# Order of instructions at three stage fronts of a one-core decoder kernel: gates of the last network moved up, attention's turned rows copied ahead of the next rows, query stack cleared behind the constants

## What is computed

```python
x = x + attn(layernorm(x))            # L0, L1: causal, 16 heads of 8, rotary; L2: channel attention; L3: state space
x = x + xattn(layernorm(x), ctx)      # L0 (gated), L1, L3: 16 heads over the context; L2: decay mixing
x = x + ffn(layernorm(x))             # L0, L1, L2: one of 8 experts per token
                                      # L3: shared network plus 2 of 8 small experts, by sigmoid scores
```

## Time and profile before

| what | value |
|---|---|
| median of 3 runs | 1519.24 us (1514.60 to 1520.48) |
| profiled execution, its own time | 1520.62 us |
| its span in the trace | 1518.8 us, 30086 instructions |
| PE, DVE, ACT, POOL busy | 78%, 64%, 42%, 39% of the span |
| granted clock of PE, mean | 0.871 |

### The profile page before, as it was taken

One profiled execution on the slowest core, in us unless ns is written; L12 is line 12 of the kernel. 1 busy time (PEld: TensorE's weight loads), 2 busy tenths in 40 slices (PEclk: granted clock), 3 DMA queues, 4 the chain that ended last, 5 costly groups with the idle time before them and its releaser, 6 DMA issues. The chain is left out here.

```text
span 1518.8 us, 30086 instructions
## 1 busy us (share of the span) xinstructions
PE 1187.3 (78%) x9187; PEld 788.5 (52%) x9187; DVE 977.1 (64%) x4100; ACT 640.3 (42%) x1541; POOL 597.9 (39%) x1132
## 2 busy tenths in 40 slices
PE   3789999998465478999997495874758865999778
PEld 2456555554365245565553394663655642454455
DVE  6677777774666567787772674456665755775445
ACT  2256555444222135566654043331335431666422
POOL 3554478987243344355520443322430122321120
PEclk8699999999578579999999597876887886999889
DMA  6344765530022344455420125001220014331000
GB/s 187 111 131 126 218 198 166 182 116 12 32 60 62 98 125 127 134 172 166 148 93 12 41 57 177 0 15 38 62 74 1 0 39 146 99 121 39 2 0 28
DMA packets 140015, 137.35 MB, mean 90 GB/s; under 512 B 12289, under 2 KB 109185, under 8 KB 139729
## 3 DMA queue, kind: packets, MB, share of 16 engines
q1 hardware_dynamic: 131248, 110.88, 24.0%
q0 software_dynamic: 8608, 24.55, 5.0%
HBM read 83.58 MB, written 49.18 MB: 87 GB/s over the span
## 5 line engine op out<-in xcount | busy, mean ns | idle before, releaser
L763 ACT ACTIVATE L0a_Pr<-PS 128x512 f32<-128x512 f32 (+1 forms) x256 | 137.0, 547 | 140.5 <-PE PS L665 86.4
L763 ACT ACTIVATE L1a_Pr<-PS 128x512 f32<-128x512 f32 (+1 forms) x256 | 136.2, 548 | 104.1 <-PE PS L662 51.6
L480 POOL TENSOR_TENSOR L0a_PG<-L0a_Pr,L0a_G 128x512 f32<-128x512 f32 x80 | 105.8, 1326 | 23.6 <-issue 10.4
L886 DVE CUSTOM_DVE_ANT_0 L1a_junk<-PS,L1a_neg 128x256 bf16<-128x256 f32 x256 | 94.8, 420 | 29.4 <-PE PS L638 29.1
L638 PE MATMUL PS<-L1a_Kst,Qm 128*128 128x256 bf16 (+1 forms) x512 | 94.6, 272 | 16.4 <-DVE L1a_mx L886 8.6
L638 PE MATMUL PS<-L0a_Kst,Qm 128*128 128x256 bf16 (+1 forms) x512 | 94.7, 272 | 16.1 <-DVE L0a_mx L886 9.2
L886 DVE CUSTOM_DVE_ANT_0 L1a_junk<-PS,causal_q 128x128 bf16<-128x128 f32 (+1 forms) x256 | 78.4, 353 | 38.4 <-PE PS L638 37.6
L886 DVE CUSTOM_DVE_ANT_0 L0a_junk<-PS,causal_q 128x128 bf16<-128x128 f32 (+1 forms) x256 | 78.4, 353 | 38.1 <-PE PS L638 37.5
L660 PE MATMUL PS<-Qm,L0a_Kst 128*128 128x512 bf16 (+1 forms) x256 | 91.2, 356 | 12.2 <-DMA Qm<-L0a_mT 9.5
L660 PE MATMUL PS<-Qm,L1a_Kst 128*128 128x512 bf16 (+1 forms) x256 | 91.2, 356 | 10.5 <-DMA Qm<-L1a_mT 7.3
L889 DVE TENSOR_REDUCE L3x_mx<-PS 128x2 f32<-128x512 f32 x128 | 83.6, 687 | 24.2 <-PE PS L638 23.7
(11 more groups left out here) (739 smaller groups left out, 3189.8 us busy)
## 6 DMA issues: line engine op xcount, KB each, us to landing
Qm<-q_image SPq DMA_DIRECT2D x160, 128.0 KB
sorted_in<-zeros POOLq DMA_DIRECT2D x16, 516.0 KB, 4.3
L0a_Kst<-k_image SPq DMA_DIRECT2D x64, 128.0 KB
ffn_w_<-L_ffn POOLq DMA_DIRECT2D x32, 256.0 KB, 3.5
L1a_Kst<-k_image SPq DMA_DIRECT2D x64, 128.0 KB
ffn_w_<-L_ffn SPq DMA_DIRECT2D x16, 256.0 KB, 6.5
L3x_Kst<-k_image SPq DMA_DIRECT2D x32, 128.0 KB
k_image<-L0a_kpart SPq DMA_DIRECT2D x16, 192.0 KB, 2.5
```

The source lines that it names most:

```text
L480: g.tensor_tensor(PG[:, V_ % GATED_RING, :].rearrange("p (h q) -> p h q", h=2), Pr[:, V_ % RING, :].rearrange("p (h q) -> p h q", h=2), G[ ...
L763: a(Pr[:, V_ % RING, 0:2 * nq], PS[:, T_BANK + v % 2, 0:2 * nq], ACT.Exp, scale=SCALE)\
L886: ins = v.tensor_tensor_reduce(junk[:, tt, par, 0:nk], scored[:, par], off, 1.0, LOWEST, ALU.add, ALU.max, mx[:, i % 2, tt, par, hp:hp + 1])
```

## The change

Three edits of order; no instruction is added or removed. In attention, ACT's copy of the turned rows (XT+1) stands ahead of the writing of normalised rows (NORM+1) within a slot. In the first pass, DVE's second clear of Qm moves from its first instructions to behind the constants. In the last network the fourth turn moves from unit 5 to unit 4, the gate products from units 2, 4, 6, 7 to 2, 3, 4, 5, and the exponential from before unit 9 to before unit 7.

```diff
--- before.py
+++ after.py
@@ -785,6 +785,12 @@
                         if i >= RUNS:
                             act.wait_ge(s["xn_ready"], i - RUNS + 1)
                         a(r0[:, i % RUNS], lnv[:, i % RUNS], ACT.Exp, scale=-0.5).then_inc(s["ln_r0"], 1)
+                    i = at(n, XT + 1)
+                    if i is not None:
+                        act.wait_ge(s["xT_psum"], i + 1)
+                        if i >= DEPTH:
+                            act.wait_ge(s["v_psum"], i - DEPTH + 1)
+                        a(xT[:, i % DEPTH], PS[:, f_bank(XT), 0:S], ACT.Copy).then_inc(s["xT_ready"], 1)
                     i = at(n, NORM + 1)
                     if i is not None:
                         act.wait_ge(s["ln_scale"], i + 1)
@@ -794,12 +800,6 @@
                             ins = a(xn[:, i % 2, t, :], tile(items[i][1], t), ACT.Identity, scale=rstd[:, i % RUNS, t:t + 1],
                                     bias=shift[:, i % RUNS, t:t + 1])
                         ins.then_inc(s["xn_ready"], 1)
-                    i = at(n, XT + 1)
-                    if i is not None:
-                        act.wait_ge(s["xT_psum"], i + 1)
-                        if i >= DEPTH:
-                            act.wait_ge(s["v_psum"], i - DEPTH + 1)
-                        a(xT[:, i % DEPTH], PS[:, f_bank(XT), 0:S], ACT.Copy).then_inc(s["xT_ready"], 1)
                     i = at(n, K + 1)
                     if i is not None and items[i][0] not in ROPE:
                         first_part(i, "k", f_bank(K))
@@ -904,7 +904,6 @@
 
                 if first:
                     v.memset(Qm[0:64, :, 1], 0.0).then_inc(s["setup"], 1)
-                    v.memset(Qm[64:P, :, 0], 0.0).then_inc(s["setup"], 1)
                 for n in SLOTS:
                     if first and n == CONSTS:
                         dve.wait_ge(s["w_in"], 16)
@@ -912,6 +911,7 @@
                             v.tensor_copy(to[:, :], w(name))
                         v.memset(core.causal_q[:, 0:P], 0.0)
                         v.tensor_copy(core.causal_q[:, P:S], w("neg_q")).then_inc(s["consts"], 1)
+                        v.memset(Qm[64:P, :, 0], 0.0).then_inc(s["setup"], 1)
                     i, u = unit(n, 0)
                     if i is not None:
                         if first and i == 0 and u == 0:
@@ -2313,9 +2313,9 @@
     N = len(units)
     count = lambda kind, n: sum(1 for u in units[:n] if u[0] == kind)
     nth = lambda kind, g, k: units.index((kind, g, k))
-    TURN_AT = {1: 1, 3: 2, 5: 3}
-    GATE_AT = {2: 0, 4: 1, 6: 2, 7: 3}
-    SIGMOID_AT = 9
+    TURN_AT = {1: 1, 3: 2, 4: 3}
+    GATE_AT = {2: 0, 3: 1, 4: 2, 5: 3}
+    SIGMOID_AT = 7
     MASK_AT = {nth(SHARED, 2, NE - 1): 0, nth(ROUTED, 0, 1): 1, nth(ROUTED, 1, 1): 2, nth(ROUTED, 2, 1): 3}
     spread = [("mask", g) if x == "mask" else ("pick", x) for n in range(N) for x, g in
               ([(n, None)] if units[n][0] == ROUTED else []) + ([("mask", MASK_AT[n])] if n in MASK_AT else [])]
```

## The result

The changed kernel took 1506.94 us (median of 5 runs, 1506.00 to 1511.05), the kernel before 1519.32 beside it (5 runs, 1514.60 to 1520.48): a ratio of 0.9929, 95% interval 0.9909 to 0.9950. Forecast were 1509.4 and 1503.5 to 1516.0, and "faster by over 0.5%" had the largest chance. A later comparison of 9 runs with 18 of the kernel before gave 0.9943 (0.9923 to 0.9963), a third 0.9939 (0.9922 to 0.9956).

What follows compares the result with a forecast made beforehand. Bound: a chain of barrier-separated stages, where one engine's order holds back a ready product at each front. Terms 4.66+2.05+1.46+1.70=9.87 off the profiled 1520.62 make 1510.8; from the median, 1509.4, range 1503.5 to 1516.0.

Steps and rivals of the forecast that it cites:

- First front, 4.66 forecast: First pass: item 0's copy of turned rows at 9.66 instead of 14.32, 4.66 earlier, by moved clear and copy order.
- the statistics can start at 4.75, the 0.70 of idle stays: First pass, DVE: first statistics start where the memset did, 2.65 earlier, with the idle before it kept.
- the forecast's second sentence: First pass: statistics could even start at 4.05, 3.35 earlier, but POOL, on its table until after 5.89, could hardly follow.
- The clear's new place, 0 forecast: First pass: memset behind the constants delays neither item 2's statistics nor POOL's normalising; price 0, bound a loss of 2.45.
- Second network, 2.05 forecast: Second network's attention front: copy of turned rows ahead of item 1's rows gives 2.05, bounds 1.9 to 2.1.
- L3x, 1.46 forecast: L3x front: key's first part (L753) 1.46 earlier, still behind item 1's rows and a logarithm of 0.21; bounds 1.2 and 2.07.
- Last network, 1.70 forecast: Last network: routing starts 3.0 earlier, 1.3 lost to POOL's multiplies, so 1.7 gained; bounds 0.9 and 3.0.
- The walk against POOL's cadence: Last network's routing: POOL's multiplies, every 1.75, hold L2514 by 0.8 and the second L2511 by 0.5, 1.3 lost.
- The turn's wait: Last network: fourth transpose, now behind unit 4, waits 0.5 for DVE's rows; bounds 0 and 1.2.
- I leave the half clock as it is.: Last network: PE still idles about 5.0, over the 4.3 after which the clock fell, so no gain was counted.
- The rivals: Clock stays up: 1506.6 (0.12); first front gives half: 1510.4 to 1511.9 (0.12); pass swallows front: 1517.5 (0.12); slower pass: 1527 (0.06).
- the slower rival: First pass stays at half clock, keyed products 0.63 instead of 0.36; at 41 us delay 7.7 slower, 1527; chance 0.06.

## Why the prediction was right, and where its steps were off

- **First front, 4.66 forecast.** The first key product came 4.75 earlier and the image writes 4.76; the pass's fifteenth item of sixteen ended 4.57 earlier (376.28 to 371.71). The step "the statistics can start at 4.75, the 0.70 of idle stays" was off: they started at 3.98, because that idle belongs to the clear and moved with it. It hardly mattered, as the forecast's second sentence said: POOL was still on its table (6.14), so that the rows came 2.78 earlier, 0.13 beyond the 2.65. The wait ahead of the rows grew from 1.76 to 2.47.
- **The clear's new place, 0 forecast.** Right: item 2's statistics at 9.98 wait for x's load; L451 and L452 are at their 0.20 and 0.22 beside it.
- **The rest of L0a.** The pass ended 6.65 earlier in the profiled pair and 5.86 on the mean of the traces, not 4.66. The 2.1 that came on top in the pair arose between the fifteenth item's end and the sixteenth's, where the kernel before had dropped to half clock (0.74 over 376 to 388 us) and the changed one dropped only at 379.7, with its last item's products done. Over all twelve traces the fifteenth item ended 5.0 earlier, and from there to the sixteenth's end it took 8.0 or 9.6 to 10.1, in both kinds. The other 0.9 of the 5.86 is how often the long one came. No term of the sum had it.
- **Second network, 2.05 forecast.** 2.04 at the image write, 2.05 on the mean of traces.
- **L3x, 1.46 forecast.** L753 came 1.59 nearer: the logarithm that follows item 1's rows held it 0.09, not 0.21. On the mean of traces the stage gave 1.27; in the profiled one nothing, with 54.8 of half clock for 44.3.
- **Last network, 1.70 forecast.** L2401 came 1.81 nearer (38.78 after the stage's start, from 40.59). The walk against POOL's cadence was right in both places and sizes: 0.78 at L2514 and 0.52 at the second L2511, together 1.30. The turn's wait was 0.32 for 0.5, and the idle 5.00 as forecast.
- **"I leave the half clock as it is."** That step was off. The clock fell where it had (37.3 after the stage's start, 37.6 before) but rose after 6.8, not 10.2, and 5.4 after L2401 in place of 7.3. So one unit of the routed work ran at half, where in the kernel before a part of the next did too (its product began with 1.21 and ended with 0.63). It comes with edit 3: the half clock there lasted 10.2 in all four traces without edit 3, and 6.8 in all five that have it and nothing added there. It gave 0.86 more in the profiled pair (2.67 for the stage, 1.81 at L2401), and 0.5 more on the means (2.33 for the stage, 1.78 at L2401).
- **The rivals.** None came about. The forecast of 9.87 stands against 12.4, 10.1 and 9.9 by the three comparisons' medians. The first lay 2.5 beyond it. That two of them lie within 0.3 of the forecast is in part luck: each is good to about 3, and the gains that no term had come to about 1.4 on the means of traces (0.9 in L0a's tail, 0.5 behind the routing).
- **The first pass at half clock** (the slower rival): keyed scores took 0.356 on the mean, as in the earlier trace rows:

```profile
L660 PE MATMUL PS<-Qm,L0a_Kst 128*128 128x512 bf16 (+1 forms) x256 | 91.0, 356 | 12.9 <-DMA Qm<-L0a_mT 10.1
```

## What to carry to other kernels

In a program whose stages are joined by barriers, look at each front for a ready result that stands behind a later item's work in one engine's order: the order can be put right without one instruction more, and the gain at the front is read from two rows before anything is built. Where DVE's chain is what PE waits for, keep POOL's multiplies off it: six squares on ACT took 3.2 off a chain of 15.5. And compare stages over several traces before crediting an edit: here one stage of unchanged instructions differed by 3.0 between executions of one program.

## What the runs showed that was not expected

- DVE's idle of 0.70 ahead of the 64-partition clear goes with the instruction: it stands before it at 4.75 in the kernel before and at 7.17 after the change. What it is stays open.
- The clock can fall behind very little idle: after 4.46 of products, 0.70 idle ahead of L2401 and 0.86 behind it, it was at half for 3.4; behind an idle of 1.84 it fell in one trace and not in another. And it fell 37.6 after the last network's start in the kernel before and 37.3 in the changed one, though PE had stopped 4.3 before in the one and 3.5 in the other. Over the nine traces with nothing added in the last network it fell 2.5 to 4.3 after PE had stopped.
- Stages of the same instructions come in different lengths: L3a 106.9 to 107.1 in nine traces and 108.9 to 110.1 in five; L3x 175.5 to 179.8 for one order of instructions. L3x goes with the amount of half clock it catches. In L3a it isn't the amount alone: 30.2 of half clock went with a length of 107.1 in one trace, and 29.9 with 109.9 in another.
